# A two-layer decoder on one core: a written-out sequence of steps in another order around the loads of the third and fourth batch

## The reference

```
x = layernorm(x + L0_attn(x))          # 16 heads of 8, each token sees 7 neighbours
x = layernorm(x + L0_xattn(x, ctx))    # additive attention over 77 keys: w . tanh(Wx + Ws c + b)
x = layernorm(x + L0_ffn(x))           # 8 experts of 512, the best 2 of each token, silu-gated
x = layernorm(x + L1_attn(x))          # one head, 32 largest scores of each row are kept
x = layernorm(x + L1_xattn(ctx, ctx, x))
x = layernorm(x + L1_ffn(x))           # shared expert + 8 experts of 256, best 2, exact gelu
```

## Time and profile before

| | us |
|---|---|
| median of three runs | 651.83 |
| the three runs | 651.83, 652.91, 649.58 |
| the profiled execution | 653.7 |
| its span, first to last instruction | 651.9 |
| PE busy | 593.6 (91%) |
| DVE busy | 464.6 (71%) |
| ACT busy | 412.0 (63%) |
| POOL busy | 139.4 (21%) |

### The profile page before, as it was taken

The page is one execution under the profiler, slowest core; times in us unless marked ns, Lnnn a source line. Parts: engine busy times, 40 slices in busy tenths (PEclk is TensorE's granted clock), DMA queues, the critical chain, the costliest instruction groups (busy, mean ns, idle before and its releaser), DMA issues.

```text
span 651.9 us, 10832 instructions
## 1 busy us (share of the span) xinstructions
PE 593.6 (91%) x3516; PEld 384.9 (59%) x3516; DVE 464.6 (71%) x1396; ACT 412.0 (63%) x798; POOL 139.4 (21%) x136
## 2 busy tenths in 40 slices
PE   3578997879999999999999999699999999999995
PEld 1262252326556454655555666467668897888885
DVE  3746756644586737887949889968659996996744
ACT  2108998969678988689888554254564455445541
POOL 1002002320181431103664104411013111001200
PEclk9588998989999999999999999699999999999999
DMA  8931000120001130000130001300001000000000
GB/s 279 411 140 38 2 1 0 55 76 10 5 18 59 33 93 17 14 13 13 43 108 5 22 13 46 108 9 18 20 24 29 2 17 2 1 0 18 1 18 18
DMA packets 28182, 29.26 MB, mean 45 GB/s; under 512 B 4952, under 2 KB 24288, under 8 KB 27744
## 3 DMA queue, kind: packets, MB, share of 16 engines
q1 hardware_dynamic: 26080, 24.36, 11.3%
q0 software_dynamic: 2048, 4.20, 2.3%
HBM read 19.51 MB, written 9.04 MB: 44 GB/s over the span
## 4 chain that ended last, share of the span: by engine, by line
PE 67%; issue 6%; DVE 3%; ACT 3%; POOL 1%; DMA 1%; POOLq 0%; SPq 0%; DVEq 0%; ACTq 0%
PE bank L887 16%; PE bank L903 8%; PE bank L805 7%; PE bank L1044 7%; PE bank L894 4%; PE bank L984 2%; PE bank L961 2%; PE bank L776 2%; PE bank L699 2%; PE bank L700 2%; PE bank L701 2%; PE bank L879 1%; PE bank L977 1%; POOL x_rows L1754 1%; PE bank L858 1%
## 5 line engine op out<-in xcount | busy, mean ns | idle before, releaser
L1122 ACT ACTIVATE a_big<-feat,txt_cols 128x512 f32<-128x512 f32 x252 | 162.1, 713 | 4.6 <-PE bank L805 4.3
L887 PE MATMUL bank<-gup_sb,x_cols 128*128 x240 | 125.5, 609 | 0.5 <-ACT x_cols L1163 0.4
L805 PE MATMUL bank<-a_big,score_pad 128*32 128x512 f32 x616 | 103.6, 625 | 3.7 <-ACT a_big L1122 3.1
L1237 ACT ACTIVATE a_big<-bank,cols_sb 128x512 f32<-128x512 f32 x72 | 49.2, 688 | 56.6 <-PE bank L701 55.8
L1527 DVE SCALAR_TENSOR_TENSOR gated_sb<-gated_sb,bank 128x256 f32<-128x256 f32 x120 | 50.0, 417 | 43.9 <-ACT gated_sb L1188 43.3
L903 PEld LDWEIGHTS bank<-down_sb,hid_sb 128*128 128x128 f32 x480 | 62.3, 191 | 31.6 <-issue 31.6
L1044 PEld LDWEIGHTS bank<-rw_sb,a_big 128*128 128x128 f32 x576 | 69.4, 192 | 2.8
L1044 PE MATMUL bank<-rw_sb,a_big 128*128 128x128 f32 x576 | 69.9, 275 | 0.0
L903 PE MATMUL bank<-down_sb,hid_sb 128*128 x480 | 64.0, 276 | 2.6 <-ACT hid_sb L1170 2.6
L1188 ACT ACTIVATE gated_sb<-bank 128x256 f32<-128x256 f32 x120 | 45.9, 383 | 29.8 <-PE bank L887 29.1
L1720 POOL TENSOR_TENSOR b_rstd<-b_var,neg_half 128x4 f32<-128x4 f32 x16 | 16.4, 1023 | 182.2 <-DVE b_var L1268 182.2
(11 more groups left out here) (280 smaller groups left out, 1002.7 us busy)
## 6 DMA issues: line engine op xcount, KB each, us to landing
gup_sb<-gup SPq DMA_DIRECT2D x1, 4096.0 KB, 15.5
y_rows<-x_tiles SPq DMA_DIRECT2D x60, 64.0 KB, 1.5
down_sb<-down SPq DMA_DIRECT2D x1, 2048.0 KB, 17.3
x_rows<-b_y SPq DMA_DIRECT2D x2, 960.0 KB, 10.4
x_tiles<-x_rows SPq DMA_DIRECT2D x4, 448.0 KB
rw_sb<-rw SPq DMA_DIRECT2D x1, 1152.0 KB, 19.6
a_qT<-x_T SPq DMA_DIRECT2D x4, 256.0 KB, 2.6
a_tok<-x_tok SPq DMA_DIRECT2D x4, 256.0 KB, 3.0
```

Source lines behind the costliest of these rows:

```text
L805: last = mm(P[2][32 * j:32 * j + 32, :], score_pad[:, 31 - i:63 - i], ring[k % RING], start=(i == 0), stop=(KCOL * (i + 1) + j >= KEYS))
L887: mm(P[3 + h][:, :], x_col[i % 2], part[:, bass.ds(at_of[i], I0)], start=True, stop=True)\
L1122: act(ring[(k + j) % RING], feat[b][:, :], ACT.Tanh, bias=txt_cols[:, c:c + 1])\
L1237: act(hid6[u % 2][:, c * S:(c + 1) * S], P[5 + n % 2][:, :], ACT.Gelu, bias=col("rb1", n))\
```

## The change

`SUMS` and `SEQUENCE` are replaced; nothing else. `SUMS` gives the sum of a pair to another engine here and there: in batch 0 from 17 pairs on DVE and one on POOL to 20 on DVE and none on POOL; in batch 1 from none to one on each; in batch 2 from one DVE and four POOL to three and two; in batch 3 from one and four to two and five. That is 28 pairs summed beforehand against 34. Otherwise the steps are the same, and the engines get them in another order:

- DVE, start: `split.0` stands between `product.0.1` and `product.0.2`, before it stood behind `product.0.3`; `split.2` moves from batch 1's `spread` to batch 0's.
- POOL: `input.2` and `input.3` stand ahead of `scatter.0` and `scatter.1`, before behind them. SP: `load_a.3` is three steps earlier.
- Batch 2's rows: `place.2.1` directly behind `place.2.0` on DVE, and with it `scatter.2` on POOL.
- Batch 3's rows: on DVE `halves.0` before `gate.2.19`, `top.1.0.1` before `place.3`; on PE `keys.1` after `half.2.28`, `kscore.1.2` and `kscore.1.3` before `half.2.31`, and `context.1.0` between `half.2.32` and the first step on batch 3's rows (`half.3.-1`), before it was behind `half.3.1`; `key_sums.1` behind `half.3.2`.
- In the last stage `context.2.0` and `context.3.0` stand directly ahead of `context.2.2` and `context.3.2`.

The table, and the parts of the sequence that this text speaks of:

```diff
-SUMS = (" vvv vvgv      vvv   vvvvv v v       v  ",
-        "                                        ",
-        "vggg g                                  ",
-        "               g g g             vg     ")
+SUMS = (" vvv vvvv      vvv   vvvv vv   v  vv v  ",
+        "                       g             v  ",
+        "vvgg               v                    ",
+        "             g g g         v     vg  g  ")
...
-project.0 product.0.0 product.0.1 product.0.2 product.0.3 value.0 input.0 split.0 split.1 score.0 rows.0 to_tokens.0
-shift.0.0 shift.0.1 exp.0 probability.0 to_rows.0 rest.0 spread.0.0 spread.0.1 blend.0.0 spread.0.2 blend.0.1
+project.0 product.0.0 product.0.1 split.0 value.0 product.0.2 product.0.3 score.0 rows.0 split.1 input.0 to_tokens.0
+shift.0.0 shift.0.1 exp.0 probability.0 to_rows.0 rest.0 spread.0.0 spread.0.1 blend.0.0 spread.0.2 split.2 blend.0.1
...
-gate_apply.0 norm_a.0.2 load_a.2 rprrprr turn_x2.0 p logits_x2.0 rank.0.0 rrp rank.0.1 positions.0 place.0.0 rr
-place.0.1 r share_exp.0 share.0 rpr project.2 product.2.0 product.2.1 product.2.2 pr scatter.0.0 value.2 prr
+norm_a.0.2 turn_x2.0 rp logits_x2.0 rr rank.0.0 p load_a.2 rank.0.1 r positions.0 place.0.0 share_exp.0 rrpr place.0.1
+share.0 project.2 rp value.2 product.2.0 rp product.2.1 product.2.2 product.2.3 rr score.2 input.2 rp rows.2
+to_tokens.2 scatter.0.0 scatter.0.1 scatter.0.2 scatter.0.3 r load_rows.0.0 load_rows.0.1 load_rows.0.2 load_rows.0.3
...
-rank.1.0 tp rank.1.1 gtrgr positions.1 place.1.0 p load_a.3 r place.1.1 scatter.1.0 tgr project.3 product.3.0 tg
+gate_sums.1.2 pgtrgrt pow.1 gate_apply.1 pgrtpg norm_a.1.2 tg load_a.3 trg turn_x2.1 tgrr logits_x2.1 t rank.1.0
...
-rank.3.1 g halves.0 tg positions.3 t place.3.0 place.3.1 gtgt top.1.0.1 scatter.3.0 g scatter.3.1 tg kscore.1.2
-scatter.3.2 scatter.3.3 top.1.0.2 tgt keys.1 key_sums.1 top.1.0.3 gtg load_ctx.2 tg kept.1.0 load_rows.3.0
-load_rows.3.1 load_rows.3.2 load_rows.3.3 kscore.1.3 tg top.1.2.0 top.1.2.1 tt top.1.2.2 share_exp.3 gg context.1.0
+rank.3.0 tgt rank.3.1 gtgt share_exp.3 top.1.0.1 gtg positions.3 place.3.0 place.3.1 tgtg keys.1 t scatter.3.0
+scatter.3.1 top.1.0.2 g top.1.0.3 tg scatter.3.2 scatter.3.3 kscore.1.2 kscore.1.3 kept.1.0 tgtg gather.2.0 gather.2.1
+gather.2.2 gather.2.3 load_rows.3.0 context.1.0 load_rows.3.1 load_rows.3.2 load_rows.3.3 tg top.1.2.0 top.1.2.1
```

More of the change, by code:

```diff
@@ L113 @@
[L113 to L117, removed]
@@ L118 @@
[L118 to L122, removed]
@@ L133 @@
[L133 to L137, removed]
@@ new lines @@
+shift.0.0 shift.0.1 exp.0 probability.0 to_rows.0 rest.0 spread.0.0 spread.0.1 blend.0.0 spread.0.2 split.2 blend.0.1
+spread.0.3 blend.0.2 blend.0.3 output.0 norm_a.0.1 turn.0 feature.0 fp.0 rsrsprsrpr load_a.1 srsrs project.1 rpsr
+product.1.0 product.1.1 product.1.2 r value.1 prrpr product.1.3 score.1 rpp rows.1 rsrsrs to_tokens.1 input.1 rpr
+shift.1.0 shift.1.1 p exp.1 rrs probability.1 rp to_rows.1 psrsr rest.1 srr spread.1.0 psrsr blend.1.0 p spread.1.1 rp
+blend.1.1 rprsrr spread.1.2 rpsrs spread.1.3 blend.1.2 prr blend.1.3 srpp output.1 rp norm_a.1.1 rho_rows.0 rho_turn.0
@@ new lines @@
+spread.2.2 rpgprr spread.2.3 blend.2.0 p blend.2.1 rrp blend.2.2 blend.2.3 rrrr output.2 tgptprsr norm_a.2.1 r turn.2
+gpp feature.2 rho_rows.1 fp.2 stgr rho_turn.1 rho_shift.1 stg rho_exp.1 tg gate_sums.1.0 tg gate_sums.1.1 trsgtrs
+gate_sums.1.2 pgtrgrt pow.1 gate_apply.1 pgrtpg norm_a.1.2 tg load_a.3 trg turn_x2.1 tgrr logits_x2.1 t rank.1.0
+rank.1.1 pgrtgr positions.1 place.1.0 place.1.1 trg share_exp.1 project.3 input.3 scatter.1.0 pr product.3.0
+product.3.1 tgpr scatter.1.1 scatter.1.2 scatter.1.3 product.3.2 tgprr product.3.3 score.3 rrp rows.3 rspr to_tokens.3
@@ new lines @@
+shift.3.0 value.3 shift.3.1 tgt exp.3 probability.3 rtggpr to_rows.3 tpgrtg rest.3 spread.3.0 tr blend.3.0 g
+load_rows.1.0 prr load_rows.1.1 gather.0.0 gather.0.1 load_rows.1.2 load_rows.1.3 spread.3.1 p gather.0.2 r gather.0.3
+spread.3.2 rrtgprr blend.3.1 tpg spread.3.3 blend.3.2 rrrprtt combine.0.0 gpgr blend.3.3 rt output.3 gpr norm_a.3.1
+rtppg rho_rows.2 combine.0.1 tg turn.3 rho_turn.2 rho_shift.2 tg rho_exp.2 t norm_b.0.1 feature.3 g fp.3 tg
+gate_sums.2.0 tg gate_sums.2.1 gate_sums.2.2 pow.2 turn_b.0.1 tgrtgr kq.0 gate_apply.2 tg share.1 v1.0 trgr kscore.0.0
@@ new lines @@
+tg norm_a.2.2 kscore.0.1 pt top.0.0.0 prgrtg top.0.0.1 tgr turn_x2.2 tpgt logits_x2.2 rg rank.2.0 t rank.2.1 rgtprp
+top.0.0.2 grtrpgt share_exp.2 top.0.0.3 positions.2 rs place.2.0 r place.2.1 gprsr kscore.0.2 tgrs kept.0.0 tgpr
+kscore.0.3 top.0.2.0 scatter.2.0 r scatter.2.1 tgrptg keys.0 r top.0.2.1 tg scatter.2.2 trgprtgpr scatter.2.3 tgtg
+gather.1.0 gather.1.1 context.0.0 top.0.2.2 r load_rows.2.0 top.0.2.3 kept.0.2 load_rows.2.1 load_rows.2.2 rp
+context.0.2 load_rows.2.3 rsrtpgrp kout.0 gather.1.2 key_sums.0 load_ctx.1 rt norm_b.0.2 r gather.1.3 t turn_b.0.2
@@ new lines @@
+kscore.3.0 kscore.3.1 u keys.3 u top.3.0.0 u top.3.0.1 uuu top.3.0.2 u top.3.0.3 uu halves.2 uuuu kscore.3.2 u weigh.2
+uu kscore.3.3 u kept.3.0 top.3.2.0 top.3.2.1 top.3.2.2 top.3.2.3 kept.3.2 uuu key_sums.3 store.0 context.3.0
+norm_b.1.4 context.3.2 u kout.3 uu norm_b.3.2 turn_b.3.2 u xscore.3 xshift.3 xexp.3 u residual.3.2 xturn.3 u xout.3
+xsum.3 uu xadd.3 u norm_b.3.3 turn_b.3.3 router.3 halves.3 route.3 route_exp.3 uu residual.3.3 weigh.3 uuuu norm_b.2.4
+uuuuuuuu store.1 uuuuu store.2 uuu norm_b.3.4 store.3
```

33 lines of the change are left out of this document (14 added, 19 removed).

## The result

The changed kernel takes 653.45 us at the median of 20 runs against 651.83 for the kernel before (20 runs). The ratio is 1.0027, 95% interval 1.0016 to 1.0038: 1.8 us slower, 1.0 to 2.5. A second comparison gave 1.0031 (1.0015 to 1.0047). That is less than 0.5%, but both intervals lie wholly on the slower side. The time lies inside the stated range of 645.0 to 655.0, but the forecast of 649.5 had the wrong sign. Yet the profiled execution of the kernel after took 653.36 us (span 651.6), beside 653.7 for before: these two profiles, taken alone, show the changed kernel slightly ahead. Most of this case lies in that contradiction.

What follows compares the result with a forecast made beforehand. PE was taken as the bound, busy 593.6 of 651.9 us, so only places where it waits were priced. The terms +1.9, 0, -1.3, +0.75, -0.7, -3.0 and 0 sum to -2.35: median 649.5 us, range 645.0 to 655.0.

Steps and rivals of the forecast that it cites:

- Split.0: Start, batch 0: split.0 ahead of the last products delays score and the whole chain, +1.9 us.
- split.2: Moved from batch 1's spread to batch 0's on DVE: fits into idling, 0; up to +1 if its piece lands late.
- Sums: Batch 0's sums: POOL's pair goes to DVE, so ACT's idles of 0.92 and 0.38 go, -1.3 us.
- Input.2: input.2 and input.3 ahead of the scatters: r_top waits for POOL's addition on the way to batch 0's slots, +0.75 us.
- Batch 1's rows: PE's idle of 0.90 at 233.62 for ACT's hid_sb shrinks as one key's tanh stands behind, -0.7 us.
- The last stage: context.2.0 and context.3.0 behind further up steps: DVE's kept blocks are last and PE has filling work, 0.
- Batch 3's rows: Fourth load: context.1.0 fills PE's wait and context.1.2 begins earlier, despite rows 1.4 later, -3.0 us.
- B: Rival, chance 0.18: batch 3's late rows are bare, +1.4 there, and ACT's gains fail; sum +4.05, median 655.9.
- A: Rival, chance 0.26: at the fourth load PE keeps its full clock, -5.5 in place of -3.0; median 647.0.
- C: Rival, chance 0.16: nothing at all, the sums make up the start's loss; -0.6 to +0.5, median 651.8.

Runs made afterwards that it cites:

- e3: The kernel before with the new order from rank.3.0 to kout.1 alone: 1.0034 against the kernel before, +2.2 us.
- e4: The changed kernel with the old order from rank.3.0 to kout.1, halves.0 keeping its new place: 0.9999 against the kernel before, -0.1 us.
- f1: The combined kernel f2, but with the new order from rank.3.0 to kout.1: 0.9962 against the kernel before, -2.5 us.
- f2: Old start, new sums and batches, inputs behind scatters, old fourth-load order with context.1.0 early, new last stage: 0.9955 against the kernel before, -2.9 us.
- e1: The kernel before with the new order up to batch 0's fp step alone (split.0 and split.2 moved): 1.0029 against the kernel before, +1.9 us.
- e12: The kernel before with split.0 alone moved, ahead of product.0.2: shift 10.07 us behind the first product, against an expected 8.20 in before.
- f3: The combined kernel f2 with top.1.2.3 and kept.1.2 ahead of gate.3.0 and gate.3.1 on DVE: 1.0021 against the kernel before, +1.4 us.
- e8: The changed kernel with input.2 and input.3 behind the scatters again: r_top at 0.18 us; its one time, 650.19 us, is a single run.
- f4: f1 with positions.3 and place.3 at the old place, ahead of gate 25, top behind gate 26: 0.9949 against the kernel before, -3.3 us.
- e6: The kernel before with batch 3's slots late, behind one round of top and two gates: 1.0029 against the kernel before, +1.9 us.
- e2: The changed kernel with the old order at the start alone: 0.9985 against the kernel before, -1.0 us.
- e9: The changed kernel as it is, run again on another chip: 1.0031 against the kernel before, +2.0 us.
- e5: The kernel before with context.1.0 alone moved, ahead of the first step on batch 3's rows: 1.0007 against the kernel before, +0.5 us.
- e7: The same combined kernel as f2, in an earlier comparison: 0.9968 against the kernel before, -2.1 us.
- e10: The changed kernel with positions.3 and place.3 early, behind gate 24, the round of top right behind them: 1.0041 against the kernel before, +2.7 us.
- e11: Probe: combined kernel e7 with two top rounds over 64 columns, leaving out 4.4 us of DVE's work: 0.9950 against the kernel before, -3.3 us.

## Why the prediction was wrong

Point by point, by its own terms:

- *Split.0, +1.9*: right. Column A is 7.93 to 8.21 with the old start and 10.05 to 10.07 with the new one; split.2 cost nothing that shows.
- *Sums, -1.3*: right. Column B has a mean of 52.09 over the six kernels with the old sums and of 50.8 over the others. The row that I named moved as I had said: in the changed kernel the mask instruction takes 0.24 in place of 1.25, and ACT no longer idles 0.92 behind it (the idle of 0.38 ahead of it stayed, 0.37). No run moved the sums apart from the other steps of this stretch.
- *Input.2, +0.75*: right, +0.8 (20.00 to a mean of 20.8).
- *Batch 1's rows, -0.7*: about right. From the first to the third load the stretch is 193.02 before and 192.43 after, -0.6; PE's idle of 0.90 at 233.62 is gone. No run tested this step by itself.
- *The last stage, 0*: missed a gain of 0.44. Column F is 214.42 to 214.47 with the old stage and 213.98 to 214.08 with the new one. It shows at one step, where PE's transposes L858 take 1.01 in before and 0.60 in after; why, stays open.

- *Batch 3's rows, -3.0*: this is the step that failed. Without it my own terms, with the missed one, sum to +1.9 - 1.3 + 0.75 - 0.7 - 0.44 = +0.2; 1.8 was measured, which leaves +1.6 for this place. Its direct measurements are +2.2 (e3, within 0.6 to 3.9), about +1.8 (after less e4), and +0.4 (f1 less f2, against an order with `context.1.0` early). By the profiles, E has a mean of 38.5 in the four kernels with the old order and of 38.6 in the six with the new one, while `r_top` itself comes 0.7 later behind the third load (column C: 64.1 to 64.3 with the old place of `halves.0`, 64.9 to 65.2 with the new one ahead of it). That step counts in E in the one and in C in the other, so C and E together are the fair stretch: 102.8 in the mean of the four and 103.5 in that of the six. So the place is worth between nothing and +2, and no gain.

Why it failed has two parts. First, and shown best, the gain was measured from one execution. I took what the low clock had cost in rows 10 and 11 as a cost of this order of steps. The table shows that most of it isn't: in four executions of the old order at this place the low clock lasted 10.2, 3.4, 3.4 and 6.8 us, and E was 40.36, 37.54, 37.56 and 38.53. `context.1.2`, which I wanted 3.0 us earlier, began 33.66 behind `r_top` in the profile that I had, and 30.84 and 30.87 behind it in e1 and e12, with the same steps at this place. The profile that I had was the worst of the four, and 2.8 us of its E, nearly all of my 3.0, came with the extra 6.8 us at 1.2 GHz. Comparing the two profiles repeats the error, for between the same two instructions they differ by 2.3 in favour of the new order (40.36 and 38.09), as if the step had been right, and over 20 runs nothing of it is left. The mean granted clock, which is on record for every execution, tells how far apart the two profiles were: that of before has 0.961, and of the 122 executions of that kernel in the later comparisons none was lower (mean 0.967, up to 0.971); that of the changed kernel has 0.969, and none of its 32 was higher (mean 0.967, down to 0.963). In the mean the two kernels don't differ; the two profiles stand at opposite ends. As an estimate: the spans of the two profiles differ by -0.3, and with the mean E of either order (38.5 and 38.6) in place of theirs by +2.0, where 20 runs of each say +1.8.

Second, what the early `context.1.0` closes opens again behind it. DVE reaches the kept block of `context.1.2` only behind the gates of batch 3's first tile, so later rows make a later kept block. In the changed kernel gates wait 1.39 for the tile, the block follows at 425.44, and PE waits 1.04 for it. Even with early rows (f2) the wait of 2.95 comes back as 1.38 and 1.30, and f3 shows that neither can be bought off with the other. I had written that DVE's block would come at 422.3 to 423 and left it there; I didn't ask what it waits for. At equal low clock, C and E together are 101.7 twice for the old order, 102.4 and 103.2 with `context.1.0` early, and 103.0, 103.0 and 103.6 with the new order (3.4 us); 103.4 against 104.8 and 105.4 (6.8 us). That is a loss of 1.3 to 2.0, and it agrees with the +1.6 that the sum leaves. Where the clock didn't fall (0 us), the new order with late rows (e8, 101.3) was no slower than early rows with `context.1.0` early (f2 and f4, 101.5); the old order was never caught there, and these are single executions. How the loss divides between late rows, low clock and the moved steps stays open.

That lateness I had about right, by a wrong reason. Against `r_top`, the slots are 3.2 later (7.84, 4.62; I had 3.5) and the load 1.45 later (column D; I had 1.3). But I wrote that the scatters released the load before, and it was the store of the last tile, with the scatters some 2 us ahead of it. e6 shows the price of the late slots alone, +1.9 us; by the trace of before, slots up to 2 us later would not have moved the load (an estimate: 4.47 from the last scatter to the load there, 2.25 where the scatter released it).

Of the rivals, B named the right term, late rows that nothing covers, and its +1.4 for the place is close. Its point of decision (`kept.1.0` behind 412.4) was not the one, since that block's two halves were ready at 410.9 and 411.5, and its condition that the sums gain nothing didn't hold. A was drawn from the same single execution as the forecast. C came nearest in time (651.8), but its range of -0.6 to +0.5 is passed: the sums didn't make up for the start and `input.2`, +1.9 and +0.8 against -1.3. The Trainium skill ("TensorE: Matmul & The Clock Gate", section "HAM oscillation — how this bites in real kernels") says of a kernel with a DMA wait ahead of each piece of matmul work that each piece starts at the low clock. The traces agree in part. Before, after, e1, e12, e4, e6, e2 and e3, with waits for the rows of 2.05 to 5.26, show the low clock at the end of the wait or within 2 us of it. But e8, e9 and f1, with waits of 1.93 to 2.00, don't: e8 shows none, and e9 and f1 have it some 10 us later, as e5 and e7 do, with no wait for rows. These are single executions, and the changed kernel itself stands on both sides (as after and as e9): the order of steps doesn't alone choose when the clock falls. On `r_top`, the rule that the Trainium skill gives in "SBUF — State Buffer", section "SBUF: two separate sides", would have given 0 by its case of two SBUF inputs, and a stop by its case of a 2-port mode; the trace decides for a stop until POOL's end, 1.03 against 0.18, and no run here shows the mode.

## What to carry to other kernels

Before a stall is priced, find out how much of it belongs to the order of work and how much to that one execution: a stretch in which the granted clock changes should be seen in several executions, cut between the same two instructions, or be charged with its idle time alone. When a load waits for two things, find the later one and the slack of the other, because a move that eats it changes the releaser. And on a full engine in program order (DVE here), ask of every step what stands ahead of it and waits: closing PE's wait for rows only exposed the gate and the kept block behind it.

## What the runs showed of the hardware

- A one-input TENSOR_SCALAR on DVE over 128x32 f32 took 0.84 to 1.13 us in place of 0.18 when it met POOL's TENSOR_TENSOR of 1.26 (the changed kernel, e2, e4, e9 and e10), ending 0.03 to 0.04 behind it each time, and 0.18 in the 13 other traces, where POOL's instruction stood elsewhere.
- The low clock behind the fourth load lasted 0, 3.4, 6.8 or 10.2 us in executions with nearly or exactly the same steps (e7 and f2 are one kernel, with 3.4 and 0), and went with 36.4 to 36.7, 37.5 to 38.7, 38.5 to 40.8 and 40.4 us for the same stretch E (e10, e11 and f3 left aside). By pairs with the same steps there (before and e1, after and e8, e7 and f2) that is an estimated 0.4 to 0.5 us lost for each us at 0.50.
- From the start of the last indirect scatter's instruction to the load that waits for it there were 2.24 to 2.25 us in the changed kernel (412.64 to 414.89), e6, e8, e9 and f1, but 2.91 in e2 and 3.30 in e3. From the store of a tile to the load that waits for it there were 1.65 to 1.67 us in all eleven traces where the store was last.
